# Graph attention layer on one core: high parts of eight last tiles for the bound D, g and p's scale by exp from d, and the first group's orders written anew

## The reference

```python
def _L0_gnn_ref(x, adj, W, a1, a2):
    h = x @ W.T
    src = h @ a1
    dst = h @ a2
    e = jax.nn.leaky_relu(src[:, None] + dst[None, :], negative_slope=0.2)
    e = jnp.where(adj == 0, jnp.float32(-9e15), e)
    attention = jax.nn.softmax(e, axis=1)
    return attention @ h

h = jnp.maximum(_layernorm(x, axis=-1), 0.0)
return x + _L0_gnn_ref(h, adj, W, a1, a2)
```

## Time and profile before

| what | us |
|---|---|
| median of 3 runs | 384.66 (383.9 to 385.73) |
| the profiled execution | 384.0 |
| its span, first to last instruction | 382.4 |
| TensorE, VectorE, ScalarE, GpSimd busy | 376.6, 362.8, 195.7, 43.1 |
| mean granted TensorE clock | 1.000 |

### The profile page before, as it was taken

How to read it: one execution, slowest core, us unless ns; L and a number is a source line. 1 busy time by engine, 2 the same in 40 slices (tenths; PEclk the granted TensorE clock), 3 DMA queues, 4 the chain that set the end, 5 groups by cost and what they waited for, 6 DMA issues and landing times.

```text
span 382.4 us, 9231 instructions
## 1 busy us (share of the span) xinstructions
PE 376.6 (98%) x3358; PEld 330.5 (86%) x3358; DVE 362.8 (95%) x456; ACT 195.7 (51%) x272; POOL 43.1 (11%) x68
## 2 busy tenths in 40 slices
PE   8999899999999999999999999999999999999996
PEld 6788688888888888888888888888888888888885
DVE  4999999999999999999999999999987999999965
ACT  5999754744443644344445543444446443444430
POOL 3897020000000001110000002100000011100001
PEclk9999999999999999999999999999999999999999
DMA  7931476857676666776666667766665567666503
GB/s 252 374 78 42 136 228 223 278 165 233 221 222 215 210 218 221 235 231 224 220 218 205 216 209 234 239 222 222 216 208 184 169 216 244 232 219 225 171 2 111
DMA packets 27025, 78.23 MB, mean 205 GB/s; under 512 B 3956, under 2 KB 9336, under 8 KB 27000
## 3 DMA queue, kind: packets, MB, share of 16 engines
q1 hardware_dynamic: 25568, 74.59, 60.4%
q0 software_dynamic: 1280, 3.16, 2.2%
q10 hardware_dynamic: 152, 0.13, 0.1%
HBM read 73.66 MB, written 4.21 MB: 204 GB/s over the span
## 4 chain that ended last, share of the span: by engine, by line
PE 96%; ACT 1%; DMA 1%; issue 1%; DVE 0%; ACTq 0%
PE ps L1435 88%; PE ps L1259 2%; PE ps L1274 2%; PE ps L1285 2%; PE ps L1280 2%; DMA a_rows<-a 1%; PE ps L1224 1%; PE ps L1240 1%; ACT c_row L517 0%; ACT h_sb L491 0%; DVE rows_sb L1153 0%; ACT L643 0%; ACT p_hi L527 0%; ACTq L502 0%; PE ps L1234 0%
## 5 line engine op out<-in xcount | busy, mean ns | idle before, releaser
L1435 PE MATMUL ps<-v_sb,p_hi 128*128 (+2 forms) x2048 | 251.9, 273 | 1.0 <-ACT p_hi L527 0.9
L537 ACT ACTIVATE p_hi<-p_sb,gp 128x1024 f16<-128x1024 f32 x126 | 144.4, 1149 | 166.5 <-DVE p_sb L816 140.0
L1435 PEld LDWEIGHTS ps<-v_sb,p_hi 128*128 128x128 f16 x2048 | 199.6, 98 | 26.9 <-issue 1.2
L823 DVE SCALAR_TENSOR_TENSOR p_lo<-p_sb,gp,p_hi 128x1024 f16<-128x1024 f32 x126 | 160.7, 1277 | 7.2 <-ACT p_hi L537 6.7
L816 DVE SCALAR_TENSOR_TENSOR p_sb<-c_row,gp,adj_sb 128x1024 f32<-128x1024 uint32 (+1 forms) x126 | 160.5, 1278 | 0.0
L1435 PE MATMUL ps<-v_sb,p_lo 128*128 (+1 forms) x1024 | 141.6, 273 | 0.0
L1435 PEld LDWEIGHTS ps<-v_sb,p_lo 128*128 128x128 f16 x1024 | 100.0, 98 | 12.8 <-DVE p_lo L823 0.2
L467 POOL DMA_DIRECT2D out<-rows_sb x24 | 13.0, 541 | 263.0 <-DVE rows_sb L1117 262.9
L416 POOL TENSOR_SCALAR hn_sb<-x_sb,moments,rstd 128x256 f32<-128x256 f32 x17 | 21.3, 1260 | 4.1 <-DVE rstd L765 3.2
L775 DVE SCALAR_TENSOR_TENSOR hnt_lo<-ps,hnt_hi 128x256 f16<-128x256 f32 x32 | 12.9, 410 | 0.3 <-ACT hnt_hi L507 0.2
L1274 PE MATMUL ps<-w_hi,hnt_hi 128*128 128x258 f16 x64 | 12.5, 277 | 0.4 <-ACT h_sb L491 0.4
(11 more groups left out here) (87 smaller groups left out, 87.9 us busy)
## 6 DMA issues: line engine op xcount, KB each, us to landing
adj_sb<-adj_t SPq DMA_DIRECT2D x128, 512.0 KB, 4.8
x_sb<-x SPq DMA_DIRECT2D x7, 512.0 KB, 8.5
out<-rows_sb POOLq DMA_DIRECT2D x24, 128.0 KB, 4.6
...
```

Source lines behind the costliest of these rows:

```text
L537: nc.scalar.activation(p_hi[:, u % R, :], p_sb[:, u % R, :], ACT.Copy, scale=p_scale[:, bass.ds(t, 1)])\
L823: nc.vector.scalar_tensor_tensor(out=p_lo[:, u % R, :], in0=p_sb[:, u % R, :], scalar=p_scale[:, bass.ds(t, 1)], in1=p_hi[:, u % R, :], op ...
L1435: return nc.tensor.matmul(ps[:, k, 0:width], part[:, u % R, k * P:(k + 1) * P], v_sb[:, bass.ds(t, 1), v, 0:width], start=start, stop=stop ...
```

## The change

LATE becomes 8, in two spreads of SPREAD = 4 tiles: `exp_bias` needs no kept d of tiles 24 to 31, but two `spread_d` and two reductions (`top_of`), joined by way of `d_so_far`. `gp_args` goes: ScalarE takes g and p's scale by exp straight from the d column, with `exp_bias` and `p_bias` as biases (`exp_g`, `exp_p`), which needs a fourth column of `exp_scale`. GpSimd makes `wa_norm` and all of `exp_scale` after its last normalise and no longer at the start. h has three banks (6, 7, 4), transposes three and no longer four. GpSimd normalises 19 tiles (17 before), VectorE 3 (1), ScalarE 10 (14). The orders of all engines up to the end of the first group are others; ScalarE makes no high values in the prologue, and VectorE makes `value_lo` of tiles 8 to 31 in the first group (12 to 31 before, 10 just ahead of it).

```diff
-    LATE = 4
+    LATE = 8
+    SPREAD = 4
-    BY_VECTOR = [26]
-    BY_SCALAR = [0, 1] + list(range(4, 14, 2)) + [15, 19, 21, 23, 24, 25, 29]
-    BY_GPSIMD = [2] + list(range(3, 15, 2)) + [14, 16, 17, 18, 20, 22, 27, 28, 30, 31]
+    BY_VECTOR = [24, 25, 26]
+    BY_SCALAR = [1, 4, 6, 9, 10, 12, 16, 18, 20, 21]
+    BY_GPSIMD = [0, 2, 3, 5, 7, 8, 11, 13, 14, 15, 17, 19, 22, 23, 27, 28, 29, 30, 31]
-    HIGH_BY_SCALAR = [2, 6] + list(range(14, T, 2))
-    HIGH_BY_GPSIMD = [0, 4, 8, 10, 12]
+    HIGH_BY_SCALAR = [8, 10, 14, 16, 18, 22, 26, 28, 30]
+    HIGH_BY_GPSIMD = [0, 2, 4, 6, 12, 20, 24]
...
-        bank_h = 6
-        banks_t = (2, 3, 1, 0)
+        banks_h = (6, 7, 4)
+        banks_t = (2, 3, 1)
...
+            def exp_g(t0, t1):
+                act.wait_ge(c_bias_ready, 1)
+                act.wait_ge(h_kept, t1)
+                nc.scalar.activation(g_col[:, t0:t1], h_sb[:, t0:t1, F + 1], ACT.Exp,
+                                     bias=exp_bias[:, 0:1], scale=exp_scale[:, 1:2]).then_inc(g_ready, 1)
+
+            def exp_p(t0, t1):
+                act.wait_ge(p_bias_ready, 1)
+                act.wait_ge(h_kept, t1)
+                nc.scalar.activation(p_scale[:, t0:t1], h_sb[:, t0:t1, F + 1], ACT.Exp,
+                                     bias=p_bias[:, 0:1], scale=exp_scale[:, 3:4]).then_inc(p_scale_ready, 1)
...
+            def top_of(m):
+                dve.wait_ge(d_spread, m + 1)
+                nc.vector.tensor_reduce(d_top[:, m:m + 1], ps[:, bank_d, 0:SPREAD * P], AX.X, ALU.max).then_inc(d_top_ready, 1)
...
+            def spread_d(m):
                 pe.wait_ge(w2_ready, 1)
-                pe.wait_ge(hnt_hi_ready, T)
-                a = SOON % RT * P
+                t0 = SOON + m * SPREAD
+                pe.wait_ge(hnt_hi_ready, t0 + SPREAD)
+                if m > 0:
+                    pe.wait_ge(d_top_ready, m)
...
+            def high_sums(t, m):
...
+                    if t == 0 and k in banks_h:
+                        pe.wait_ge(*kept(max(i for i in range(T) if banks_h[i % HB] == k)))
```

More of the change, by code:

```diff
@@ L641, in _ @@
             split_hn_hi(31)
-            keep_h(27)
             nc.scalar.activation(table_ready[:], eps_sb[:], ACT.Exp)
-            keep_h(28)
+            keep_h(24)
+            keep_h(25)
+            keep_h(26)
+            exp_g(0, R)
             exp_c(0)
-            keep_h(29)
-            exp_gp(slice(0, R), 1)
             exp_c(1)
             exp_c(2)
+            keep_h(27)
+            keep_h(28)
+            exp_p(0, R)
+            exp_c(3)
             hi_part(0, 0)
-            exp_c(3)
@@ new lines, in _ @@
+            turn(0)
+            turn(1)
+            project_hi(0)
+            project_w_lo(0)
+            turn(2)
+            project_hi(1)
+            project_lo(0)
+            project_w_lo(1)
+            turn(3)
+            project_hi(2)
+            project_hi(3)
+            project_lo(1)
+            turn(4)
+            project_w_lo(2)
+            turn(5)
+            project_lo(2)
+            project_w_lo(3)
+            project_lo(3)
+            turn(6)
+            project_hi(4)
@@ new lines, in _ @@
+            turn(28)
+            project_w_lo(23)
+            project_lo(22)
+            project_lo(23)
+            turn(29)
+            project_hi(24)
+            turn(30)
+            spread_d(0)
+            turn(31)
+            project_hi(25)
+            turn_d()
+            project_w_lo(24)
+            project_hi(26)
+            spread_d(1)
+            project_w_lo(25)
+            project_lo(24)
+            project_lo(25)
+            project_w_lo(26)
+            project_lo(26)
```

713 lines of the change are left out of this document (338 added, 375 removed).

## The result

Measured, the changed kernel takes 385.74 us (median of 16 executions) against 384.18 for the kernel before (16): a ratio of 1.0072, with a 95% interval from 1.0053 to 1.0091. Forecast was 384.7, no change. The 16 values do not lie around one time, and this has to be said to read the median: ten lie between 384.97 and 385.77, and six between 388.8 and 390.1, while the 16 of before all lie between 383.69 and 385.73. So two things have to be explained: the usual executions are 1.45 us longer than before, and about one in three is 3 to 4.5 us longer again. The six long ones lift the median by only 0.1 us (the median of the ten usual ones is 385.64).

A forecast was written before the change was run, and what follows sets the result against it. VectorE's first group was taken as the bound: first weights 1.3 us earlier, 1.4 us more work and waits behind them, so +0.1 us. From the shown median of 384.66 this gave 384.7 us, range 382.9 to 386.6.

The forecast's parts named there:

- step 3: GpSimd's normalises before the first weights: the last one, tile 31, ends at 34.0 us against 34.91.
- collisions put at 0.6 us: GpSimd's last five normalises, slowed beside VectorE's normalises and value_lo: 0.6 us in all, as before the change.
- step 1: VectorE's work and waits behind the first weights, to the first group's end: 1.4 us more.
- new waits put at 0.3: VectorE in the first group: weights_part(0, 3) waits for ScalarE's exp_c(3), +0.3 us.
- The frame: Time is the end of VectorE's first group plus a constant; groups 1 to 3 move as a block.
- step 2: From GpSimd's last normalise to the first weights: 4.0 us instead of 4.4; exp_bias ends 3.1 us after that normalise.
- Both new waits: Ahead of exp_bias: value_lo(6) for GpSimd's cast, exp_bias for exp_scale; cost nothing, 0.3 and 0.7 us spare.
- The undisturbed part: GpSimd's twelve normalises and one cast from batch 4 on, without collisions: 15.2 us from about 18.1, ending at 33.3.
- bound of 2.7: Upper bound on GpSimd's collision loss: five normalises each losing 0.54 us, 2.7 us in all.
- the likeliest case: The forecast itself: 384.7 us, own range 383.6 to 385.8, chance 0.65.
- The collisions' rival: GpSimd's last five normalises each lose 0.54 us, the last ending at 36.1: median 386.8 us, chance 0.11.
- the ring of three: VectorE's slips pass through TensorE's turns and splits to GpSimd: 0.3 to 1.0 us, 385.0 to 385.7; chance 0.13.

The follow-up runs named there:

- x10: Changed kernel with four filling matmuls ahead of turn(1) and VectorE's value_lo(0), (2), (4) moved behind top_of(0): 385.9 us (one execution).
- x1: The changed kernel run again without any edit: 385.72 us, ratio 1.0067 to the kernel before; its profiled execution is a long one.
- x4: Changed kernel with GpSimd's late casts of tiles 12, 20 and 24 moved to ScalarE inside the first group: 385.76 us, ratio 1.0076.
- x9: Changed kernel with filling matmuls ahead of turn(1), value_hi(6) and (8) on ScalarE before split_hn_hi(31), value_lo(6) and (8) earlier on VectorE: 384.83 us.
- x6: Changed kernel with normalise(1) again ahead of split_hn_hi(0) on ScalarE: 385.48 us, ratio 1.0034, no long execution.
- x7: Kernel before with normalise(1) behind split_hn_hi(0) on ScalarE: 385.51 us, ratio 1.0057; five executions at 384.23 to 384.70, five at 386.33 to 389.99.

## Why the prediction was wrong

Two terms of the sum were too small. The larger is N, the end of GpSimd's last normalise, in step 3: 0.85 us, through collisions put at 0.6 us that were 1.24 and a wait that was left out. The other is the stretch behind the first weights in step 1: 0.46 us, through new waits put at 0.3 that were 0.6. The frame and step 2 were right.

- **The frame held.** Groups 1 to 3 moved as a block, VectorE had 0.3 us of idle time in the 85.7 of the first group, and the kernel moved by what the end of VectorE's first group moved: 1.43 against 1.42 at TensorE's low sums.
- **Step 2 held.** exp_bias ended at 37.68 + 0.21 = 37.89, N + 3.04 (foretold N + 3.1), and the first weights stood at N + 4.05 (N + 4.0). Both new waits cost nothing, though exp_scale was ready at 37.54 and not at N + 2.2 = 37.05: a spare of 0.14 us and not of 0.7. value_lo(6) had none of its 0.3 either: VectorE came to the second reduction at 36.65, where the spread (35.95 + 0.59 us) was just ready.
- **Step 3 failed, by 0.85 us.** N was 34.85 and not 34.0. The undisturbed part was 0.2 to 0.3 short (N = 33.68 in x10 against 33.3 + 0.1): "without a hole if rstd keeps ahead" did not hold, GpSimd waited 0.43 us for rstd of batch 6 ahead of 27.52. The collisions, put at 0.6 us "again", were 1.24 (7.33 against x10's 6.09). The prediction had the mechanism, the rows and a bound of 2.7, and took the old sum over. Counting partners would not have given it: before had four value_lo beside its last four normalises for 0.6 us, after has three beside five for 1.2. The difference is that all three start within 0.2 us of a normalise's start, of the four in before only one. The prediction also counted VectorE's normalises as partners; x10 shows that they cost GpSimd 0.05 us at most.
- **The rule it cited** (the Trainium skill, page "SBUF — State Buffer", section "Who interferes with whom") agrees in kind: two-input value_lo held GpSimd up in after and no longer in x10, and who started first by over 0.1 us mostly went through unhindered. The traces do not bear out that the other is locked out for the whole instruction: a value_lo that began 0.15 us into a normalise of 1.22 us lost 0.26 (x1), and those of before that began 0.77 and 0.84 us into one took their usual 0.68, with 0.06 lost by the normalise. The prediction said that before's trace shows no held-up row on VectorE; after has one, the first weights with 0.70 us against 0.48 in x4.
- **Step 1 was 0.4 us short.** The stretch was 85.76 us and not 85.3 (83.96 before). From the first weights to split_lo of tile 2 VectorE took 8.68 us (38.90 to 47.58) against 8.29 (39.27 to 47.56), with 0.3 us of gp_args gone and p_bias in: its new waits, foretold at 0.3 us, came to 0.6: the foreseen one for exp_c(3) (in after it passes mostly as the longer first weights, see x4), and one of 0.20 for p_hi of tile 2 ahead of 47.58, which x9 ends by taking value_hi(8) out of ScalarE's way. About 0.1 us is not placed. The price of a value_lo, 0.60, is borne out by x9, whose stretch is 0.9 shorter: one value_lo, the wait of 0.20 and 0.1 more.
- **The sum:** 0.85 for N, 0.05 for the first weights behind it and 0.46 for the stretch make the 1.36 us by which VectorE's group ended later than the 123.3 foretold (124.66). The usual time of 385.6 lies inside the likeliest case's own range, 383.6 to 385.8, at its edge. Part of that is luck: the sum said +0.1 us, and 384.7 came from the median of three executions, 384.66, where the median of 16 is 384.18. The collisions' rival, at five losses of 0.54, would have been too much. 385.6 also lies in the range of the ring of three, 385.0 to 385.7, but its mechanism is not in the trace: the timelines of after show no wait of GpSimd from 18.09 to 27.1 and none of TensorE from 12.2 to 34.
- **The long executions were in no rival.** The prediction read ScalarE's order only for the work that it moves and not for where TensorE waits in its first microseconds. The swap of split_hn_hi(0) and normalise(1) is in the diff, and in the usual executions it costs little (0.15 to 0.3 us by x6, 0.46 by x7's five); in a third of them it is worth 3 to 5 us.
